# Graph layer pair on one core: the sort dealt over eleven tiles, indices taken in place, counts and first run at their own steps

## The reference

```python
def _rgcn(x, edge_index, edge_type, weight, root, bias):
    msgs = x[src]
    out = x @ root + bias
    for r in range(weight.shape[0]):                 # 8 relations
        mask = (edge_type == r).astype(x.dtype)
        sums = segment_sum(msgs * mask[:, None], dst, num_segments=n)
        cnt = segment_sum(mask, dst, num_segments=n)
        out = out + (sums / maximum(cnt, 1.0)[:, None]) @ weight[r]
    return out
u = _rgcn(...)
z = concatenate([u, x], axis=1) @ w_gate + b_gate
x1 = layernorm(x + tanh(u) * z + x * (1.0 - z))
# second layer: self loops, symmetric norm
h = x1 @ W
out = segment_sum(h[src] * (dinv[src] * dinv[dst])[:, None], dst, n) + b
return layernorm(x1 + relu(out))
```

## Time and profile before

| What | us |
|---|---|
| median of 3 runs | 1829.86 (1816.71 to 1838.13) |
| the profiled execution | 1797.81 |
| its span, first to last instruction | 1796.0 |
| TensorE matmul busy | 1669.5 (93%) |
| VectorE busy | 1052.9 (59%) |
| GpSimd busy | 888.6 (49%) |
| ACT busy | 565.9 (32%) |
| mean granted clock of TensorE | 0.971 |

### The profile page before, as it was taken

How to read it: one execution, slowest core, us unless ns; L and a number is a source line. 1 busy time by engine, 2 the same in 40 slices (tenths; PEclk the granted TensorE clock), 3 DMA queues, 4 the chain that set the end, 5 groups by cost and what they waited for, 6 DMA issues and landing times.

```text
span 1796.0 us, 22772 instructions
## 1 busy us (share of the span) xinstructions
PE 1669.5 (93%) x7621; PEld 1352.8 (75%) x7621; DVE 1052.9 (59%) x1937; ACT 565.9 (32%) x923; POOL 888.6 (49%) x879
## 2 busy tenths in 40 slices
PE   7999999905999999999999999999999879999997
PEld 6888888704777777888888888878878667777786
DVE  4446300005665766477777762878688885555486
ACT  3221111201333333354544542545455431111000
POOL 0008777776777772366656531767577421121000
PEclk9999999957999999999999999999999889999999
DMA  6313333220122122567666634676666642443643
GB/s 222 112 48 95 96 96 96 50 54 27 39 86 83 45 86 89 205 204 226 179 216 206 185 109 169 199 231 201 194 210 201 224 153 91 153 152 111 260 154 106
DMA packets 115115, 254.30 MB, mean 142 GB/s; under 512 B 25061, under 2 KB 25436, under 8 KB 114870
## 3 DMA queue, kind: packets, MB, share of 16 engines
q0 software_dynamic: 39904, 89.23, 18.1%
q1 hardware_dynamic: 41142, 92.41, 15.1%
q10 hardware_dynamic: 33952, 71.20, 10.6%
HBM read 185.13 MB, written 77.80 MB: 146 GB/s over the span
## 4 chain that ended last, share of the span: by engine, by line
PE 67%; DVE 7%; issue 2%; POOL 1%; another core or an unknown queue 0%; ACT 0%; DMA 0%; DVEq 0%; ACTq 0%; POOLq 0%
PE PG L694 42%; PE PM L718 9%; PE PG L783 6%; PE PG L852 5%; PE PM L705 3%; PE PG L802 2%; DVE X L1336 1%; DVE STATS L1330 1%; DVE XLO L1071 1%; DVE X L1353 1%; DVE GATE L1352 1%; PE PM L791 1%; PE PM L772 0%; DVE TANH L1342 0%
## 5 line engine op out<-in xcount | busy, mean ns | idle before, releaser
L694 PE MATMUL PG<-WHI,XHI 128*128 128x512 f32 x1600 | 637.4, 398 | 70.1 <-DVE WLO L1071 70.1
L694 PE MATMUL PG<-WHI,XLO 128*128 128x512 f32 x1600 | 627.1, 392 | 0.0
L694 PE MATMUL PG<-WLO,XHI 128*128 128x512 f32 x1600 | 626.9, 392 | 0.0
L694 PEld LDWEIGHTS PG<-WHI,XHI 128*128 128x128 f32 x1600 | 302.5, 189 | 134.9 <-DVE WLO L1071 68.6
L694 PEld LDWEIGHTS PG<-WHI,XLO 128*128 128x128 f32 x1600 | 302.1, 189 | 63.9
L694 PEld LDWEIGHTS PG<-WLO,XHI 128*128 128x128 f32 x1600 | 302.2, 189 | 60.8
L1071 DVE TENSOR_TENSOR WLO<-WRAW,WHI 128x512 fp32r<-128x512 f32 x176 | 124.5, 718 | 225.9 <-ACT WHI L875 214.7
L611 POOL DMA_INDIRECT WORK<-y,IDX x176 | 191.8, 1090 | 121.2 <-DVE SPLO L1226 55.4
L882 ACT ACTIVATE STAGE<-PG 128x512 f32<-128x512 f32 x200 | 118.9, 594 | 410.0 <-PE PG L694 401.6
L611 POOL DMA_INDIRECT RAW<-y,IDX x176 | 192.7, 1095 | 86.5 <-DVE SPLO L1226 44.2
L536 POOL DMA_INDIRECT records<-RREC,IDX x160 | 204.6, 1279 | 61.0 <-issue 43.7
(11 more groups left out here) (168 smaller groups left out, 1897.6 us busy)
## 6 DMA issues: line engine op xcount, KB each, us to landing
y<-STAGE ACTq DMA_DIRECT2D x200, 256.0 KB
WRAW<-in_L_gnn_weight_dram SPq DMA_DIRECT2D x30, 1024.0 KB
WRAW<-in_L_gnn_w_gate_dram SPq DMA_DIRECT2D x8, 1024.0 KB
WORK<-y SPq DMA_DIRECT2D x10, 512.0 KB, 6.3
GATE<-y SPq DMA_DIRECT2D x10, 512.0 KB
x<-X ACTq DMA_DIRECT2D x10, 512.0 KB, 6.0
WORK<-x SPq DMA_DIRECT2D x10, 512.0 KB, 4.7
WORK<-in_x_dram SPq DMA_DIRECT2D x9, 512.0 KB, 3.7
```

Of the source, the lines that this page charges most:

```text
L694: last = pe.matmul(PG[:, bank, :], lhs[:, k, t * P:(t + 1) * P], rhs[:, j % 2, k, :], start=(k == 0 and n == 0), stop=(k == KT - 1 and n = ...
```

## The change

The sort's steps move into the first eleven tiles of body 0 (`sort_step`, now by `jt`), the offsets' matmuls from after tile 14 to after tile 7. GpSimd's three indirect loops take the index from ADDR or REC and the data in place; IDX, RREC, WGOT, `idx_set` and `w_ready` are gone. The stages are given by one list of steps (`spread`): setup at step 128, counts 132 to 219, run 0 226 to 313, run 1 88 pairs over steps 325 to 399.

```diff
+OFFSETS_JT = NT - 3
-COUNT_AT = (3, 0)
-RUN0_AT = (5, 20)
-RUN1_BODY = 8
-SETUP_AT = (2, 32)
-LATE = 5
+SETUP_STEP = 128
+COUNT_FROM = 132
+RUN0_FROM, RUN0_TO = 226, 314
+RUN1_FROM, RUN1_TO = 325, 400
+def spread(start, end):
+    steps = end - start
+    bounds = [k * NPAIR // steps for k in range(steps + 1)]
+    return {start + k: range(bounds[k], bounds[k + 1]) for k in range(steps)}
...
-                nc.gpsimd.tensor_copy(IDX[0:EPART, b, :], ADDR[:, col]).then_inc(idx_set, 1)
-                nc.gpsimd.tensor_copy(RREC[0:EPART, b, :, :], REC[0:EPART, col, :]).then_inc(idx_set, 1)
-                pool.wait_ge(idx_set, i * 4 + (2 * b + 2))
...
+            for c in range(ECOL):
+                b = c // RING % 2
+                if c % RING == 0:
+                    after(pool, scattered[b], c // (2 * RING) * (16 * RING))
+                    pool.sem_inc(passed_pool, 1)
+                pool.indirect_dma_start(
+                    out=rec_d, out_offset=bass.IndirectOffsetOnAxis(ap=ADDR[:, c:c + 1], axis=0),
+                    in_=REC[0:EPART, c, :], in_offset=None).then_inc(scattered[b], 16)
...
+                pool.indirect_dma_start(
+                    out=W_EDGE[:, tile:tile + 1], out_offset=None, in_=inv_d,
+                    in_offset=bass.IndirectOffsetOnAxis(ap=REC[:, tile, 1:2], axis=0),
...
+                for tile in range(ETILES):
+                    after(pool, msg_split, tile + run * ETILES - (ROWS - 1))
+                    pool.sem_inc(passed_pool, 1)
+                    pool.indirect_dma_start(
+                        out=raw[tile % ROWS], out_offset=None, in_=y_d[0:(run + 1) * YROWS, :],
+                        in_offset=bass.IndirectOffsetOnAxis(ap=REC[:, tile, 0:1], axis=0),
...
-                if jt == 14:
+                if jt == OFFSETS_JT:
+                    pe.wait_ge(x_split, 2 * (OFFSETS_JT + 2))
...
-                    act.wait_ge(w_ready, 2 * (ETILES // (2 * RING)))
+                    for b in range(2):
+                        act.wait_ge(w_got[b], 16 * (ETILES // 2))
...
+                elif jt == 1:
                     membership()
+                    scan_step(0)
+                elif jt == 2:
+                    scan_step(1)
+                    scan_step(2)
...
+                elif jt == OFFSETS_JT + 1:
                     group_starts()
                     positions_a()
-                elif n == 17:
+                elif jt == OFFSETS_JT + 2:
                     positions_b()
```

More of the change, by code:

```diff
@@ L57 @@
 AHEAD = 2
-COUNT_AT = (3, 0)
-RUN0_AT = (5, 20)
-RUN1_BODY = 8
-SETUP_AT = (2, 32)
-LATE = 5
[L67 to L119, removed]
+SETUP_STEP = 128
+COUNT_FROM = 132
+RUN0_FROM, RUN0_TO = 226, 314
+RUN1_FROM, RUN1_TO = 325, 400
+STEPS_ALL = SUBSTEPS * (UNITS_Y + 4) // 2
+def spread(start, end):
+    steps = end - start
+    bounds = [k * NPAIR // steps for k in range(steps + 1)]
+    return {start + k: range(bounds[k], bounds[k + 1]) for k in range(steps)}
+COUNT_PAIRS = spread(COUNT_FROM, COUNT_FROM + NPAIR)
+RUN0_PAIRS = spread(RUN0_FROM, RUN0_TO)
+RUN1_PAIRS = spread(RUN1_FROM, RUN1_TO)
 class Chain:
@@ L720, in message_pair, with steps @@
                 last.then_inc(pair_done, 1)
-            def steps(pair_step):
-                def step(i, s, pairs):
-                    i, s = normal(i, s)
-                    gemm(i, s // 2, s % 2)
-                    for pair, n in pairs:
-                        pair_step(pair, n)
-                return step
+            def steps(start, end, pairs={}, pair_step=None):
+                for s in range(start, end):
+                    gemm(s // SUBSTEPS, s % SUBSTEPS // 2, s % 2)
+                    for pair in pairs.get(s, ()):
+                        pair_step(pair, pair)
             pe.sem_inc(cells_done, AHEAD)
@@ L914, in take_counts, with steps @@
                                      PM[:, 2 * (n % 2):2 * (n % 2) + 2, 0:NCOL // 2], ACT.Copy).then_inc(cells_taken, 1)
-            def steps(run, counts=False):
-                def step(i, s, pairs):
-                    i, s = normal(i, s)
+            def steps(start, end, pairs={}, run=None):
+                for s in range(start, end):
                     if run is not None:
-                        for pair, n in pairs:
-                            msg_high(pair, n, run)
+                        for pair in pairs.get(s, ()):
+                            msg_high(pair, pair, run)
                     if s % 2 == 0:
-                        i, jt = (i, s // 2 - 1) if s > 0 else (i - 1, TILES_BODY - 1)
+                        i, jt = (s // 2 - 1) // TILES_BODY, (s // 2 - 1) % TILES_BODY
                         evac(i, jt)
@@ L927, in step @@
                         store_y(i, jt)
-                    if counts:
-                        for pair, n in pairs:
-                            take_counts(pair, n)
-                return step
+                    if run is None:
+                        for pair in pairs.get(s, ()):
+                            take_counts(pair, pair)
             act.sem_inc(cells_taken, AHEAD)
@@ L1276, in _ @@
             dve.wait_ge(work_clear, 1)
-            plain(phase_end(COUNT_AT), RUN0_AT, nothing)
-            def add0(pair, n):
-                msg_add(pair, n, 0)
-            def add1(pair, n):
-                msg_add(pair, n, 1)
+            steps(count_end, RUN0_FROM)
+            dve.wait_ge(dinv_ready, 1)
             dve.wait_ge(deg_max_turned, 1)
```

160 lines of the change are left out of this document (45 added, 115 removed).

## The result

The changed kernel is slower: 1949.78 us median (1945.5 to 1951.69, 4 executions) against 1823.28 us (1800.34 to 1838.13, 4 executions) for the kernel before, a ratio of 1.078 with a 95% interval of 1.069 to 1.087. That ratio takes the kernel before by its two fast executions, 1800.34 and 1816.71 us, since the other two lie over 1.5% above the fastest; by the two medians it would be 1.069. The forecast was 1774 us, a ratio of 0.969. The profiled execution took 1951.69 us, with a span of 1950.0 us and a mean granted clock of 0.929.

What follows compares the result with a forecast made beforehand. TensorE bound the kernel, with one 65.8 us hole from late sorted records. Terms -67.4 + 13 + 1.7 + 2.0 - 5 = -55.7 took the median from 1829.86 to 1774 us (profiled 1797.81 to 1742), range 1752 to 1799.

Steps and rivals of the forecast that it cites:

- the paragraph on the edge-weight lookups: GpSimd's 176 lookups start near 354, are done by 613, before the counts end at 683; no cost in the sum.
- the line on the copies that go: GpSimd's scatter rings: the two copies and their wait cost about 1.0 us per ring of eight, saved when removed.
- rival C: Slower than before: scatters taking index and record in place cost more; at 0.72 us more each, median 1858; chance 4%.
- Addresses at 86: VectorE's sort steps, moved earlier, finish the scatter addresses at 86 us, 43 us earlier than before.
- Scatters 1.48 apart: GpSimd's 160 in-place scatters come 1.48 us apart, 253 to 256 us in all with 16 to 19 extra.
- Records at 349: Sorted records reloaded and landed at 349 us against 410.8 before, 31 us ahead of the need at 380.4.
- The gain of 67.4: TensorE's 65.8 us wait before step 120 goes whole, with 1.6 us of slow restart.
- Before step 320: Between run 0 and the next, TensorE waits 2.0 us (0 to 5) for low halves queued behind VectorE's clear.
- Run 1: Second message run, now without index copies on GpSimd, wins back 5 us (0 to 10) of 12 lost.
- The wait at step 226: TensorE waits 13 us (9 to 19) for the counts' store before run 0, plus 1.7 for a fallen clock.
- the page's figure: HBM limit of about 358 GB/s per core; by it the counts' store takes 2 us more, a wait of 15.
- The forecast's own test list: Signs to check: addresses at 86, records near 349, scatters 1.48 apart, TensorE unbroken to step 226, then one 9-19 us wait.

Runs made afterwards that it cites:

- run 0: Not an experiment: the kernel's first run of message pairs, 88 pairs over steps 226 to 313 in the changed kernel; it ended at step 307 before.
- e1: Changed kernel with the 176 edge-weight lookups back through ring buffers, with copies every 8 lookups; 1739.57 us, ratio 0.973.
- e2: Changed kernel with two tiny waited-for GpSimd memsets ahead of every 8 in-place lookups; 1738.1 us, one execution.
- e7: Changed kernel with GpSimd waiting, ahead of every 8 lookups, until the 8 just issued have landed, no compute between; 1736.28 us.
- e3: Kernel before with one part of the change alone, the 176 edge-weight lookups in place without ring copies; 1998.55 us, ratio 1.114.
- e14: Changed kernel with GpSimd waiting for all landings after every 16 lookups; 1731.19 us.
- e9: Changed kernel with lookups drained (landings waited for) ahead of every 8, and run 0 from step 231 instead of 226; 1727.47 us, ratio 0.964.
- e16: Changed kernel with two lookups per pair of counts from the 17th lookup on, and run 0 from step 231; 1719.21 us, ratio 0.961.
- e6: Changed kernel without the waits on earlier landings, 176 in-place lookups issued with nothing between; 1945.37 us.
- e10: Changed kernel with GpSimd waiting for all landings after every 32 lookups only; 1944.71 us.
- e12: Changed kernel with four landing semaphores, every lookup waiting for the one four before it; 1936.6 us.
- e17: Same program as e10, changed kernel with all landings waited for after every 32 lookups, in four executions; 1947.51 us.
- e18: Changed kernel with all landings waited for and 24 waited-for memsets after every 64 lookups; 1919.93 us.
- e11: Changed kernel with one unwaited memset of one column ahead of every lookup, pace still 1.30 us; 1931.3 us.
- e13: Changed kernel with three unwaited memsets of one byte column ahead of every lookup; 1733.36 us, one execution.
- e15: Changed kernel with all landings waited for and 24 waited-for memsets after every 32 lookups; 1731.95 us.

## Why the prediction was wrong

**The step that failed** is the paragraph on the edge-weight lookups. It has them start near 354 and be done by 613, "before the counts end", and costs them at nothing; in the line on the copies that go, they count only as GpSimd's time. Their times were right (357.65 to 597.42), but not what they do to TensorE. The copies' work was indeed worth nothing, but they were also the only breaks in a row of 176 indirect DMAs, and taking them out cost 210 us on another engine, a term that the sum does not have. e1, e2 and e7 put breaks back and get 1736 to 1740 us; e3 takes them out of the kernel before and loses 206. No rival had this mechanism: rival C, on the slow side, priced the scatter in place, and the scatter was harmless.

**The steps that held.** These rows of the changed kernel are GpSimd's first scatter, two in the middle and the reload; VectorE's setup; and TensorE before step 320:

```profile
87.42 1.28 POOL L486 DMA_INDIRECT records<-REC,ADDR  x1 [81.83 <-issue]
...
200.73 1.18 POOL L486 DMA_INDIRECT records<-REC,ADDR  x1 [0.30 <-issue]
202.22 1.18 POOL L486 DMA_INDIRECT records<-REC,ADDR  x1 [0.30 <-issue]
...
349.57 0.62 POOL L492 DMA_DIRECT2D REC<-records  x1 [1.98 <-issue]
```

```profile
403.47 0.72 DVE L967 TENSOR_TENSOR WLO<-WRAW,WHI 128x512 fp32r<-128x512 f32 x1 [31.14 <-issue]
404.11 0.15 DVE L1085 TENSOR_REDUCE DEG_MAX<-DEG 128x1 f32<-128x10 f32 x1
```

```profile
1267.12 0.50 PE L599 MATMUL PG<-WHI,XHI 128*128 128x512 f32 x1 [1.72 <-DVE WLO L967]
...
1569.95 0.39 PE L623 MATMUL PM<-SPLO,ONEHOT 128*128 128x512 f32 x1
```

- Addresses at 86: GpSimd's long wait ends at 87.42. Scatters 1.48 apart: so they are, and the 160 took 260 us where 253 to 256 were taken. Records at 349: the reload is issued at 349.57 and GpSimd goes on at 352.9, so the landing was 4 us late, with 31 to spare.
- The gain of 67.4: the setup on VectorE does not wait for records (its L1085 follows the low half at once; the 31.14 us before that are TensorE's held stretch, passed on). In e14 TensorE is busy in 236 of 236 us from 378 to 614.
- Before step 320, 2.0 forecast: 1.72.
- Run 1, 5 us of gain forecast: from 1267.12 to 1569.95 + 0.39 it takes 303.2 us against 309.5, 6.3 less.
- The wait at step 226, 13 us forecast, plus 1.7 for the clock:

```profile
894.15 0.83 DVE L1121 TENSOR_TENSOR WORK<-WORK,TALLY 128x1280 int16 x1 [2.49 <-ACT TALLY L815]
910.50 2.10 DVE L1177 MEMSET WORK<- 128x512 f32 x4 [15.52 <-DMA edge_count<-WORK]
```

```profile
927.64 0.77 PE L623 MATMUL PM<-SPHI,ONEHOT 128*128 128x512 f32 x1 [15.13 <-issue]
928.20 0.63 PE L623 MATMUL PM<-SPLO,ONEHOT 128*128 128x512 f32 x1
```

TensorE waits 15.13 us, 2 more than the value taken and inside 9 to 19. The chain is the one forecast: VectorE has added the last counts at 895 and stands 15.52 us until their store has landed. The issue row of that stretch (queue of GpSimd, KB, us to landing) and one of its windows:

```profile
edge_count<-WORK POOLq DMA_DIRECT2D x1, 3200.0 KB, 15.0
```

```profile
904.00:906.00 2.00, 2.00 (x10) 1.00 1.07 454
```

The store takes 15.0 us beside the weights, against 9.7 (T + 2.0 to T + 11.7) alone: 5.3 more, where 4 were taken, 3.3 if both share, and 5.0 was the bound for weights that go first; the bound was a little low. The Trainium skill (DMA: Bandwidth & Descriptors, Specifications) gives HBM a limit of about 358 GB/s for a core. The windows of 2 us from 900 to 908 moved more, 439 to 458 GB/s each, but over the whole of the store, 895 to 910, the mean was 381, and 15, the wait that the forecast had worked out by the page's figure and passed over, is the one measured. No run shows which of the two readings set it. Behind the wait the granted clock is at half, matmuls come 0.43 us apart until 932.9 and then 0.23 again: 12 x 0.2 = 2.4 us lost. e9 and e16 tested the term by moving run 0 five steps back, and the wait before its first pair fell to 1.6 and 1.8 us. e9's span is 8.8 us shorter than e7's, on two chips; e16's is 13.5 us shorter than e14's on the same chip (1729.4 to 1715.9), but e16 spreads its lookups as well, so not all of that need be the move.

**The sum.** With breaks in the lookups the forecast's working is met: 1742 was forecast for the profiled execution, e7's took 1736.28; and the forecast's ratio of 0.969 stands against e1's 0.973 (0.968 to 0.978). One price was wrong by 210 us; the others that could be checked were off by some 2 us each at most, the store and the clock dearer, run 1 and the wait at step 320 cheaper, so that they nearly cancel.

The forecast's own test list would have found it: "TensorE unbroken from 18 to step 226" is the line that the profile contradicts first.

## What to carry to other kernels

When a change removes an engine's small waits and copies, ask what else they did: here the pauses that they made kept TensorE free, although TensorE waits for nothing of GpSimd's in that stretch and the DMA engines are nearly idle. A long row of short indirect gathers on GpSimd should be spread or drained (every 8 or 16, or two per step of the main engine, which was the fastest and steadiest form here), and a clock at half with idle time put down to "issue" is to be read beside GpSimd's timeline. A kernel that was slower as a whole can hold a good change: with lookups spread and run 0 five steps later, this one is 3.9% faster than the kernel before.

## What the hardware showed that was not expected

- A row of indirect gathers of GpSimd, 128 elements of 4 bytes each, one per 1.30 us, brings TensorE down to one matmul in 2.1 or 2.8 us from 16 to 29 us after the row's start, in every profiled execution of ten kernels (the changed one, e3 to e6, e10 to e12, e17, which is e10 again, and e18; less hard in e11, where TensorE was busy for 36 of 100 us instead of 21). TensorE's matmuls then start at multiples of 0.70 us (in e10's rows above, 1.40, 3.50 and 2.11 us apart), and the granted clock is at the lower of its two levels, 1.2 of 2.4 GHz, once the state is established.
- GpSimd is held too, though little. For the first 140 or so lookups of the held row it keeps its 1.30, while beside a free TensorE and VectorE some lookups take 1.4 to 1.9. But from 558 on in the changed kernel its lookups fall on the same grid of 0.70 us as the matmuls, 1.40 apart and 2.80 at each eighth:

```profile
560.60 1.00 POOL L508 DMA_INDIRECT W_EDGE<-inverse_count,REC  x1 [1.79 <-issue]
562.00 1.00 POOL L508 DMA_INDIRECT W_EDGE<-inverse_count,REC  x1 [0.40 <-issue]
...
573.21 1.00 POOL L508 DMA_INDIRECT W_EDGE<-inverse_count,REC  x1 [1.79 <-issue]
```

  e3 and e10 show it near their rows' ends, and e11 in places. One grid for both engines would fit something that they share when they issue; what it is, no run shows. (A gap of 2.8 to 4.7 us ahead of the 114th lookup is in every kernel, held or not.)
- The scatters of the same kernel, 160 in a row, 16 bytes to each of 125 rows, 1.48 us apart, don't do it, and neither did three one-byte memsets between lookups (e13), which changed the pace only from 1.30 to 1.32.

What stays open is the mechanism. Ruled out by runs are the in-place form, the place in the program and the landing semaphores as the cause by themselves; a backlog is ruled out by the packets' times; chance is ruled out for the changed kernel, e3, e17 and e18, whose four executions each agree within 0.5%. Whether the pace, the direction of the transfer or the instruction mix makes scatters and e13 harmless was not told apart, and why e15's rows of 32 stayed free, when the first rows of e10 and e18 were held with the same instructions, is not explained; e15 and e13 were each executed once. Two rivals stand untested: that what lies further on in the program, or where its code falls in memory, decides together with the breaks; and that the recording of the trace has part in it, since every execution on record carries a span and a granted clock.
